# The first layer norm of a three-part transformer block: statistics, transposes and copies in one staggered loop, with the copy on VectorE

## What is computed

```python
x = L0_attn_batch                                   # (8, 2048, 1024) f32
x = x + 0.5 * ffn(layernorm(x, eps=1e-5), w_gate, w_up, w_down)
x = x + attn_block(layernorm(x, eps=1e-5), Wq, Wk, Wv, Wo, omega, W1, b1, W2, b2, gamma, beta)
x = x + 0.5 * ffn(layernorm(x, eps=1e-5), w_gate, w_up, w_down)

def ffn(x, wg, wu, wd):        # int32 weights in -127..127, times 1/127; hidden 3072
    return (silu(x @ wg.T) * (x @ wu.T)) @ wd.T
def layernorm(x, eps):         # no scale or shift
    return (x - mean(x)) / sqrt(var(x) + eps)
```

## Time and profile before

| | before |
|---|---|
| runs (us) | 2434.37, 2628.36 (median 2531.36) |
| profiled execution (us) | 2434.83 |
| its span on the slowest core, core 7 (us) | 2433.3 (cores from 2409.5) |
| instructions | 31397 |
| TensorE busy | 1947.6 us, 80% |
| VectorE busy | 757.2 us, 31% |
| ScalarE busy | 593.5 us, 24% |
| DMA of w_down's cast, issue to landing | 121.5 us |

### The profile page before, as it was taken

The page is one execution under the profiler, slowest core; times in us unless marked ns, Lnnn a source line. Parts: engine busy times, 40 slices in busy tenths (PEclk is TensorE's granted clock), DMA queues, the critical chain, the costliest instruction groups (busy, mean ns, idle before and its releaser), DMA issues.

```text
span 2433.3 us, 31397 instructions; the slowest of 8 cores (2409.5 to 2433.3 us)
## 1 busy us (share of the span) xinstructions
PE 1947.6 (80%) x10480; PEld 952.4 (39%) x10480; DVE 757.2 (31%) x1797; ACT 593.5 (24%) x1398; POOL 65.4 (3%) x113
## 2 busy tenths in 40 slices
PE   1999959999214499988672989898985999969999
PEld 1444424444201255554332444444442444424444
DVE  5211212122300178888436313131315121101211
ACT  6211111111001088888327000000005311001100
POOL 1000010000100000000000000000001000000000
PEclk9999979999558799995695999999997999989999
DMA  9983064410999600000100434343436142063431
GB/s 219 120 114 92 12 92 64 95 62 1 101 116 117 99 19 27 20 2 2 35 1 2 172 136 140 110 141 114 139 139 120 25 82 82 23 104 53 104 138 52
DMA packets 81817, 199.90 MB, mean 82 GB/s; under 512 B 3840, under 2 KB 49152, under 8 KB 73472
## 3 DMA queue, kind: packets, MB, share of 16 engines
q0 software_dynamic: 42096, 82.39, 24.6%
q1 hardware_dynamic: 37264, 107.11, 13.1%
q10 hardware_dynamic: 2304, 8.39, 1.0%
HBM read 271.87 MB, written 37.75 MB: 127 GB/s over the span
## 4 chain that ended last, share of the span: by engine, by line
PE 66%; DMA 13%; another core or an unknown queue 6%; ACT 5%; DVE 4%; issue 3%; SPq 1%; POOL 0%; DVEq 0%; ACTq 0%; POOLq 0%; PEldq 0%
PE p L414 13%; PE p L394 13%; PE p L1135 9%; PE p L1167 9%; PE p L470 5%; PE p L476 5%; PE p L637 4%; DMA BufC<-wuT_i 3%; DMA BufC<-Wv_bf 2%; DMA BufC<-Wk_bf 2%; DMA BufC<-Wq_bf 2%; PE p L672 2%; DMA BufC<-wdT_bf 1%; DMA b2t_s<-b2t 1%
## 5 line engine op out<-in xcount | busy, mean ns | idle before, releaser
L394 PE MATMUL p<-fmA,BufC 128*128 128x512 bf16 x1536 | 368.4, 383 | 51.6 <-DMA BufC<-wuT_i 51.6
L414 PE MATMUL p<-fmA,BufC 128*128 128x512 bf16 x1536 | 364.9, 381 | 0.0
L430 DVE SCALAR_TENSOR_TENSOR actB<-p,tmpF 128x512 bf16<-128x512 f32 x192 | 132.8, 691 | 591.8 <-PE p L414 587.0
L470 PE MATMUL p<-BufC,actB 128*128 128x512 bf16 x768 | 292.0, 380 | 16.0 <-DMA BufC<-wdT_bf 12.0
L476 PE MATMUL p<-BufC,actB 128*128 128x512 bf16 x768 | 292.1, 380 | 0.0
L425 ACT ACTIVATE tmpF<-p 128x512 f32<-128x512 f32 x192 | 114.7, 597 | 649.7 <-PE p L394 649.7
L394 PEld LDWEIGHTS p<-fmA,BufC 128*128 128x128 bf16 x1536 | 150.7, 98 | 236.6 <-issue 58.6
L1135 PE MATMUL p<-fmA,BufC 128*128 128x512 bf16 x1024 | 224.7, 382 | 8.0 <-DMA BufC<-W_bf 8.0
L1167 PE MATMUL p<-actB,BufC 128*128 128x512 bf16 x1024 | 226.2, 379 | 4.3 <-DVE actB L1145 4.3
L414 PEld LDWEIGHTS p<-fmA,BufC 128*128 128x128 bf16 x1536 | 150.9, 98 | 183.8 <-issue 4.4
L637 PE MATMUL p<-fmA,BufC 128*128 128x512 bf16 x512 | 123.8, 385 | 114.9 <-DMA BufC<-Wq_bf 68.8
(11 more groups left out here) (107 smaller groups left out, 1727.9 us busy)
## 6 DMA issues: line engine op xcount, KB each, us to landing
BufC<-W_bf SPq DMA_DIRECT2D x64, 1024.0 KB, 5.7
BufC<-wgT_i POOLq DMA_DIRECT2D x32, 768.0 KB, 17.6
BufC<-wuT_i POOLq DMA_DIRECT2D x32, 768.0 KB, 20.9
W_bf<-W_sw POOLq DMA_DIRECT2D x2, 8192.0 KB, 141.6
BufC<-wdT_bf SPq DMA_DIRECT2D x4, 3072.0 KB, 12.1
BufC<-wdT_bf SPq DMA_DIRECT2D x12, 1024.0 KB, 10.4
wdT_bf<-wdT_i POOLq DMA_DIRECT2D x1, 6144.0 KB, 121.5
x_tm<-xin ACTq DMA_DIRECT2D x8, 512.0 KB, 22.2
```

Source lines behind the costliest of these rows:

```text
L394: e.matmul(pg[pi][:, 0:512], BufC[:, wg_off + k * 768 + hcl * 128: wg_off + k * 768 + (hcl + 1) * 128], fmA[:, k * 2048 + tt0 + tsl * 512: ...
L414: e.matmul(pu[pi][:, 0:512], BufC[:, wu_off + k * 768 + hcl * 128: wu_off + k * 768 + (hcl + 1) * 128], fmA[:, k * 2048 + tt0 + tsl * 512: ...
L430: e.scalar_tensor_tensor(actB[:, hc * 1024 + tsl * 512: hc * 1024 + (tsl + 1) * 512], pu[pi][:, 0:512], INV127, tmpF[:, pi * 512:(pi + 1) ...
L470: e.matmul(da[:, 0:512], actB[:, hc * 1024 + tl * 128: hc * 1024 + (tl + 1) * 128], BufC[:, hc * 1024: hc * 1024 + 512], start=(hc == 0), ...
```

## The change

Layer norm 1 is called with two more arguments. pipe_stagger=2 is only tested for truth, so it takes the staggered branch that layer norm 3 takes; pipe_ev_vec=True is new and puts the copy of emit_pev on VectorE. Layer norms 2 and 3 and all transfers stay as they are. From here on every line number of the changed kernel is one higher behind L208, two higher behind L498.

```diff
         def emit_outer_ln(eps, mu_store=None, rstd_store=None, src_wait=None,
                           src_tags=None, xl_wait=None, pipe=False,
-                          pipe_chunks=True, pipe_stagger=False):
+                          pipe_chunks=True, pipe_stagger=False,
+                          pipe_ev_vec=False):
...
-                if pipe:
+                if pipe and not pipe_ev_vec:
                     ev_tag[c] = (eS, op("scalar", lambda e, dst=dst, src=src:
                                         e.copy(dst, src),
                                         waits=[(eT, tr_tag[c])], inc=eS))
...
-        ln1_ev = emit_outer_ln(1e-5, pipe=True)
+        ln1_ev = emit_outer_ln(1e-5, pipe=True, pipe_stagger=2,
+                               pipe_ev_vec=True)
```

## The result

The changed kernel takes 2457.6 us (median of 9 runs) against 2434.9 for the kernel before; the ratio is 1.0093 with a 95% interval of 1.0079 to 1.0107. So it is 0.9% slower, and the interval excludes no change. (Some executions of either kernel run several per cent longer, with the cores of one or both dies at a lower granted clock; the ratios and the medians from here on leave them out, the two medians above don't, and without them those are 2457.4 and 2434.4, +23.0 us.) The profiled execution took 2454.83 us.

What follows compares the result with a forecast made beforehand. TensorE was taken to bound the kernel (80% busy, 66% of the chain), so a later first matmul moves the end: 22.7 + 2.1 - 1.8 = +23.0 us on 2434.83 gives 2457.8, range 2438 to 2480.

Steps and rivals of the forecast that it cites:

- (b): Layer norm 1: VectorE's queue stands at the first copy until the constants land, moving the first matmul by +22.7 us.
- E12: VectorE's copy of tile 12 out of PSUM in layer norm 1, forecast to start at 83.4 us.
- (a): Layer norm 1's copy out of PSUM: about 1.0 us on ScalarE, 0.69 on VectorE, next instruction 0.61 after its start.
- (c): TensorE's clock stays low in layer norm 1's transposes, so the first matmuls behind run slow: +2.1 us.
- (d): Quarter 2's weights are requested after the w_down cast has landed, so TensorE's wait for them goes: -1.8 us.
- no-change rival: Layer norm 1 starts early, but quarter 2's weights behind the cast hide the gain; time stays at 2434.8, chance 0.08.
- within 2%: The whole kernel's time differs by no more than about 2% (49 us), taken as no change; chance 0.95.
- the forecast with its variants: The summed time, or LN1's clock staying up (2455.3), or quarter 2's load staying slow (2459.6); chance 0.89.
- the hidden gain: The no-change rival: layer norm 1 ends early, quarter 2's weights absorb it; chance 0.08.
- the rest: Cases beyond those two, such as TensorE's low clock lasting through quarter 0 (2496, chance 0.03).

Runs made afterwards that it cites:

- e4_ident_first: The changed kernel with the identity matrix requested first, ahead of x, on its own semaphore; ratio 1.0012 to the kernel before.
- e3_vec_lag: The changed kernel with all statistics first again and each VectorE copy put behind the next tile's normalising; 2441.4 us, ratio 1.0043 to the kernel before.
- e10_stagger_mixed: The changed kernel with the identity requested first and copies of odd tiles and tile 14 on ScalarE; ratio 1.0056 to the kernel before.

## Why the prediction was right or wrong

- **The time.** 2457.8 predicted, 2457.4 measured; the shift is just the +23.0 forecast. That it fits so closely is in part luck. The parts, over the cores, come to 22.3 + 1.1 - 1.4 = 22.0, and the profiled execution of the changed kernel is only 20.0 us above the one before.
- **(b), the queue.** Right in each figure: VectorE was to stand from about 22 to 49.2 and stood from 21.3 to 49.22; the cycle was to be 2.85 and is 2.83; E12 at 83.4 came at 83.10; the first matmul at 87.2 came at 87.32 on the slowest core, and the mean shift over the cores is +22.3, where +22.7 was forecast. e4_ident_first and e3_vec_lag show it as the cause from two sides.
- **(a), the copy.** 0.68 to 0.69 us, next instruction 0.61 later (49.22 to 49.83), as in the earlier trace rows.
- **(c), the clock.** Right in kind, too large. The transposes stayed at 1.01 us for eight to the end (86.52), and the matmuls behind were slow at first, but fewer: 87.32 to 91.31 is 3.99 us for 16 where the earlier trace rows had 5.56. From first matmul to the end of quarter 0 it is 43.2 against 42.1 over the cores, so +1.1 in place of +2.1. The Trainium skill (TensorE: Matmul & The Clock Gate, The HAM clock gate) says that the number of slow matmuls varies from run to run. The trace shows such a spread already over the cores of this one execution: the first group of eight took between 2.42 and 3.41 us.
- **(d), what is late next.** Right: 18.7 us to landing where 18.0 to 22.1 were expected, the wait gone; it was worth 1.4 over the cores, 1.8 on the one I had read. Nothing later absorbed the rest: half 2 is requested 21.8 us later, and the remainder differs by 2.7 us, which is within the spread of single executions in the table.
- **The no-change rival.** Its mechanism exists (e4_ident_first, e10_stagger_mixed: the wait grows to 2.6 and 7.2), but its price was wrong. That the loop "would follow x" and "end near 56" overlooked that a cycle of 2.83 us is slower than x's four tiles in 9 us; even with the constants early it ends at 61.8. The 8 us that it was to free were under 3.
- **The step that failed** is the sentence "About 2% (49 us) is what a measurement of this kernel can tell from no change", and with it the 0.95 on "within 2%". No row gave that 2%. What the runs showed in its place is an interval of 0.14% either side of +0.93%, so the kernel was seen to be slower, beyond doubt. The sum itself said so: +23.0 us, where the times behind the two medians differ by 3 to 4 us within a kernel, and 0.89 of my own chances on times between 2453 and 2461. I should have called the direction: slower. The chances were also added wrongly: the forecast with its variants (0.89) and the hidden gain (0.08) alone are 0.97, not 0.95 with half of the rest. My range (2438 to 2480) was too cautious for the same reason; the runs behind the median lie between 2453.9 and 2458.0.

## What to carry to other kernels

Before an order is staggered, find the latest arrival among all that its waits need, constants included, and write down what each engine's queue has behind the instruction that waits for it. A prologue that runs "all statistics first" can be the better order when something small lands late: it puts the work that needs nothing in front of the wait. And when the start of a chain is made earlier, look for the next transfer that is queued behind a large one; here 8 us came through only once a cast in the same queue was divided, so that its first half was through before the next request. And before calling a forecast "no change", take the scatter of repeated runs as the measure of what can be seen, not a round percentage.

## What the runs showed of the hardware

The granted clock of the opening can't be read from its own column. TensorE in the changed kernel, windows (us, busy, granted clock, DMA share, GB/s):

```profile
52.00:86.00 34.00, 13.15 (x104) 1.00 1.06 139
87.00:91.00 4.00, 4.00 (x20) 1.00 0.98 106
```

The row says 1.00 for 52 to 86 us, yet eight transposes take 1.01 us there, as in layer norm 3 where the same view says 0.50; in the kernel before they fell to 0.61 within 8 us of the first. From 87 to 91 it says 1.00 too, while the first eight matmuls take 2.42 us and later groups 1.89. In the openings of these traces the durations tell the level (2.4 or 1.2 GHz) and the clock column doesn't.

The other thing is how sharply one transfer's landing depends on what is ahead of it in GpSimd's queue: the same 768 KB need 42.7 us when 6 MB of cast ahead of them are still under way for 28 us, and 18.9 when the half cast ahead of them has landed.

The third is that a wait of TensorE can lower its clock: behind the 7.70 us in e10_stagger_mixed the granted clock is 0.50, behind the 1.81 us of the earlier trace rows eight matmuls take the usual 1.89 us (L414 at 151.09).
